# How the per-token scales of a quantized FFN reach all partitions: a row in DRAM and two DMAs, in place of diagonal matrices

## The chip, the cores and the metric

The program runs on one core of a Trainium2 chip. TensorE (PE) multiplies and transposes, VectorE (DVE), ScalarE (ACT) and GpSimd (POOL) do elementwise work, and SyncE (SP) issues all DMAs of this kernel. The metric is the device time of one launch, in microseconds.

## The reference

64 sequences of 128 tokens, 256 features. A cross-attention block with 16 heads, then a feed-forward block whose two linear layers take inputs quantized to 8 bits per token and ternary weights.

```python
def act_quant(x):
    scale = 127.0 / jnp.clip(jnp.max(jnp.abs(x), axis=-1, keepdims=True), 1e-05)
    return jnp.clip(jnp.round(x * scale), -128, 127) / scale
...
    h = bit_linear(x, w1)                       # 256 -> 1024
    h = depthwise_conv1d(h.transpose(0, 2, 1), conv_w, conv_b)
    h = h.transpose(0, 2, 1)
    h = jax.nn.silu(h)
    return bit_linear(h, w2)                    # 1024 -> 256
...
x = x + xattn(_layernorm(x), ctx_768, ...)
x = x + ffn(_layernorm(x), ...)
```

The scale of `act_quant` is one number per token. The kernel computes it where tokens lie on partitions (a tile of 128 partitions by 4 sequences), but it needs it where tokens lie along the free axis, on every partition alike: the hidden layer is kept transposed, hidden channel on the partition and 4 x 128 = 512 tokens along the row.

## The kernel before, in words

The 64 sequences are worked on in 16 groups of 4. The work of one group is cut into 32 half-steps, numbered `n` 0 to 31 (and on from 32 where it runs over into the next group's time). Each engine has one long instruction stream, written out by hand: at half-step `n` of loop index `g` it does a piece of the attention of group `g` (`attend`, `scores`, `exponentials`), of the projections of group `g+1` (`project`), and of the feed-forward block of groups `g-1` and `g-2` (`finish`, called with `n` and with `n + 32`). Engines meet only through semaphores, and each runs its stream in order, SP's queue of DMA issues too. Loop indices 0, 1, 15, 16 and 17 are written out, 2 to 14 (13 of them) are a hardware loop, whose body is the same program.

The scale of the first linear layer: DVE computes `AD[0]` and `AS[0]` in `scales` at half-step 10. `AD[0]` is then made into four diagonal matrices (`DIAG`, line 761), PE multiplies a matrix of ones with them into PSUM at half-step 14 (line 497), ACT copies the result into `BC` (line 666) at half-step 15, and DVE multiplies each of the eight hidden tiles by `BC` (line 862) from half-step 15 on. PSUM bank `psF` is shared by all of `finish`, so the first matmul of the first layer (line 505) waits for that copy.

The scale of the second layer: at half-step 30 DVE reads the maxima that PE has transposed (line 876), computes `AS[1]` (line 758) and again the diagonal matrices; PE multiplies at half-step 32 (line 514), ACT copies at 33, and at half-steps 33 to 35 DVE (line 883) and POOL (line 1038) multiply the eight tiles of `H` by `BC`, DVE rounds them (line 890), and PE starts the second layer's matmuls (line 524).

Two loads matter for the change. The input `XIN` of the group after next is issued by SP at half-step 0 (line 311), when `unit_full` says that the previous `XIN` has been read; DVE needs it in the same half-step 0 (`bn_stats`, line 769), which stands ahead of line 883 in DVE's stream. The residual input `XRES` is issued at half-step 12 (line 333) and read by POOL from half-step 16 on (line 1065).

Of the kernel before, what the change touches and what calls it, by code (L numbers as in the profile page):

```python
# [27 lines left out]
P = 128  # L28
# [40 lines left out]
M_POW, M_NORM = 9, 9  # L69
M_QT, M_BC1 = 13, 14  # L70
M_F1 = 15
# [3 lines left out]
M_HMAX = M_F1 + M_TILE[-1] + M_HOFF  # L75
M_HT, M_BC2 = M_HMAX + 2, M_HMAX + 4
M_Q2 = M_HMAX + 5
# [57 lines left out]
def program(nc, x, ctxT, cipaT, Wq, Wk, Wv, Wo, bo, q_downT, q_up, k_downT, k_up, v_downT, v_up, o_downT, o_up,  # L135
            alphas, Wk_ipa, Wv_ipa, w1T, conv_w, conv_b, w2T, out):
    with ExitStack() as ctx:
# [66 lines left out]
        OUTT = H[:, 0:NB, T // 2:T]  # L204
        DIAG, HM = GB[0], GB[1]

# [39 lines left out]
        q1_scaled, q1_done = sem("q1_scaled"), sem("q1_done")  # L246
        diag_done = sem("diag_done")
        q1t_full, q1t_done, bc_full, bc_done = (sem(n) for n in ("q1t_full", "q1t_done", "bc_full", "bc_done"))
        f1_full, g_done, t1_done, t2_done, t3_done, th_done, h_done = (
# [52 lines left out]
        def _(sp):  # L302
# [83 lines left out]
        def _(pe):  # L386
# [98 lines left out]
            def finish(g, n):  # L485
                if n == M_QT:
# [6 lines left out]
                    m.then_inc(q1t_full, 1)  # L493
                if n == M_BC1:
                    pe.wait_ge(diag_done, g.count(2, 1))
                    pe.wait_ge(q1t_done, g.count(1, 1))
                    mm(psF, ONES[:].broadcast_to([P, P]), DIAG.rearrange("p b t -> p (b t)"), start=True, stop=True).then_inc(bc_full, 1)
                j = tile_at(n - M_F1)
                if 0 <= j < CT:
                    if j == 0:  # L500
                        pe.wait_ge(bc_done, g.count(2, 1))
                    else:
                        pe.wait_ge(g_done, g.count(CT, j))
                    for k in range(2):
                        m = mm(psF, W1[:, k, P * j:P * j + P], Q1T[:, k, :], start=(k == 0), stop=(k == 1))  # L505
                    m.then_inc(f1_full, 1)
                if n == M_HT:
# [3 lines left out]
                    m.then_inc(ht_full, 1)  # L511
                if n == M_BC2:
                    pe.wait_ge(diag_done, g.count(2, 2))
                    mm(psF, ONES[:].broadcast_to([P, P]), DIAG.rearrange("p b t -> p (b t)"), start=True, stop=True).then_inc(bc_full, 1)
                for c in range(2):
# [82 lines left out]
        def _(act):  # L598
# [53 lines left out]
            def finish(g, n):  # L652
# [3 lines left out]
                if n == M_COPY:  # L656
                    act.wait_ge(q2_done, g.count(CT, NB))
                    act.activation(OUTT, X2[:], ACT.Identity).then_inc(copy_done, 1)
                for c, m in enumerate((M_BC1 + 1, M_BC2 + 1)):
                    if n == m:  # L660
                        act.wait_ge(bc_full, g.count(2, c + 1))
                        if c == 0:
                            need(act, q2_done, g.count(CT, 0))
                        else:
                            act.wait_ge(g_done, g.count(CT, CT))
                        act.activation(BC[:], psF, ACT.Identity).then_inc(bc_done, 1)
                j = tile_at(n - M_F1 - M_LAG[0])
# [59 lines left out]
        def _(dve):  # L727
# [20 lines left out]
            def scales(g, i, clip, levels, worth):  # L748


                step = lambda k: dve.wait_ge(quant[i], g.count(4, k))
                step(1)
                dve.tensor_scalar(AM[i][:], AR[i][:], clip, None, ALU.max).then_inc(quant[i], 1)
                step(2)
                dve.tensor_scalar(AD[i][:], AM[i][:], worth, WD[:, i:i + 1], ALU.mult, ALU.mult)
                dve.reciprocal(AR[i][:], AM[i][:]).then_inc(quant[i], 1)
                step(3)
                dve.tensor_scalar(AS[i][:], AR[i][:], levels, None, ALU.mult).then_inc(quant[i], 1)
                step(4)
                for b in range(NB):  # L760
                    m = dve.tensor_scalar(DIAG[:, b, :], IDF[:], (AD if i == 0 else AS)[i][:, b:b + 1], None, ALU.mult)
                m.then_inc(diag_done, 1)

# [43 lines left out]
            def finish(g, n):  # L807
# [27 lines left out]
                if n == M_NORM + M_SCALE:  # L835
                    need(dve, h_done, g.count(CT, 0))
                    scales(g, 0, CLIP, 127.0, 1.0 / 127.0)
# [18 lines left out]
                if 0 <= j < CT:  # L856
                    dve.wait_ge(f1_full, g.count(CT, j + 1))
                    if j == 0:
                        dve.wait_ge(bc_done, g.count(2, 1))
                    if j >= 4:  # L860
# [17 lines left out]
                for j in range(CT):  # L878
                    if n == M_Q2 + j // 3 and j % 3 < 2:
                        dve.wait_ge(bc_done, g.count(2, 2))  # L880
                        if j >= 4:
# [109 lines left out]
        def _(pool):  # L991
# [37 lines left out]
            def finish(g, n):  # L1029
# [3 lines left out]
                for j in range(CT):  # L1033
                    if n == M_Q2 + j // 3 and j % 3 == 2:
                        pool.wait_ge(bc_done, g.count(2, 2))
                        if j >= 4:
# [76 lines left out]
```

## Time and profile before

| | us |
|---|---|
| median of 3 runs | 1683.01 |
| lowest and highest | 1680.71 to 1685.13 |
| span of the profiled execution | 1677.3 |

The span goes from the first to the last instruction; the times of whole runs are taken around it and lie 3.4 to 7.8 above it. The profile's own rows, below, give for each engine the time in which it was busy, the chain of work that ended last, and, for one group, the instructions in order of time. The loop's groups repeat each other closely, so one is read for all.

### The profile page before, as it was taken

How to read it: one execution, taken by the hardware profiler on the slowest of the kernel's cores; microseconds unless marked ns; L12 is line 12 of the kernel's file. 1: busy time of each engine (PE TensorE's matmuls, PEld its weight loads, DVE VectorE, ACT ScalarE, POOL GpSimd, SP SyncE). 2: the span in 40 equal slices, each digit the busy share in tenths (PEclk: the TensorE clock that was granted, in tenths of full speed). 3: DMA queues.
4: the chain of work that ended last, by engine and by line, in shares of the span. 5: the costliest groups of instructions: out<-in, count | busy, mean ns of one | idle time of the engine just before them, and what ended most of it. 6: DMA issues, size and time to landing. Idle time of an engine off the chain costs nothing.

```text
span 1677.3 us, 33155 instructions
## 1 busy us (share of the span) xinstructions
PE 1469.8 (88%) x10540; PEld 1161.8 (69%) x10586; DVE 1310.7 (78%) x3159; ACT 1183.0 (71%) x3925; POOL 729.7 (44%) x1086
## 2 busy tenths in 40 slices
PE   6999998989899998989999998989999898998642
PEld 2578877777777777777777777777777777776521
DVE  5254698887879888887979888787988888787976
ACT  2277786968778696867778696877869686776621
POOL 0125444454444544453444444444454445444510
PEclk8699999999999999999999999999999999999955
DMA  6300100000010100000010000001010000000000
GB/s 186 116 28 15 29 15 28 15 26 27 13 39 13 40 13 27 14 26 27 13 40 13 28 13 26 27 13 39 13 40 13 27 13 26 27 1 27 1 13 13
DMA packets 41128, 47.13 MB, mean 28 GB/s; under 512 B 3008, under 2 KB 35200, under 8 KB 41088
## 3 DMA queue, kind: packets, MB, share of 16 engines
q1 hardware_dynamic: 41088, 46.62, 9.1%
q8 instruction: 22, 0.36, 0.1%
q14 instruction: 18, 0.15, 0.0%
HBM read 36.13 MB, written 10.49 MB: 28 GB/s over the span
## 4 chain that ended last, share of the span: by engine, by line
PE 34%; DVE 33%; ACT 20%; issue 12%; SPq 1%; DMA 0%; DVEq 0%; POOL 0%; ACTq 0%; POOLq 0%
ACT SM L647 8%; DVE GBS L872 7%; PE PS L467 6%; PE PS L429 4%; PE PS L445 4%; PE PS L524 4%; PE PS L410 4%; PE PS L454 3%; PE PS L480 3%; PE PS L419 3%; DVE GBS L883 2%; ACT H L672 2%; DVE GBS L862 2%; ACT GBS L677 2%; DVE H L890 2%
## 5 line engine op out<-in xcount | busy, mean ns | idle before, releaser
L1026 POOL TENSOR_TENSOR SM<-SM,RC 128x496 f32<-128x496 f32 (+1 forms) x512 | 337.0, 679 | 728.8 <-DVE RC L798 728.8
L647 ACT ACTIVATE SM<-PS,MX 128x124 f32<-128x124 f32 x1024 | 359.2, 365 | 199.3 <-DVE SM L804 196.1
L467 PE MATMUL PS<-KT,QM 128*128 128x128 f32 x2048 | 279.2, 279 | 26.4 <-ACT SM L647 26.3
L467 PEld LDWEIGHTS PS<-KT,QM 128*128 128x128 f32 x2048 | 249.3, 192 | 42.6 <-ACT SM L647 41.5
L1058 POOL TENSOR_TENSOR OTl<-OF,OTh 128x256 fp32r<-128x256 f32 x256 | 216.1, 844 | 5.6 <-ACT OF L641 5.6
L647 ACT ACTIVATION_READ_ACCUMULATOR SM<-PS,MX 128x1 f32 x1024 | 210.8, 206 | 0.0
L454 PE MATMUL PS<-IDF,SM 128*128 128x128 f32 x1024 | 168.5, 287 | 18.8 <-POOL SM L1026 18.8
L639 ACT ACTIVATE OTh<-PS 128x256 fp32r<-128x256 f32 x256 | 99.5, 389 | 101.8 <-PE PS L445 98.1
L802 DVE TENSOR_REDUCE MX<-PS 128x4 f32<-128x496 f32 x256 | 170.2, 665 | 0.0
L445 PE MATMUL PS<-PT,V 128*64 128x128 f32 x2048 | 168.8, 286 | 0.0
L445 PEld LDWEIGHTS PS<-PT,V 128*64 128x64 f32 x2048 | 106.8, 136 | 82.4 <-issue 75.5
L633 ACT ACTIVATE PT<-PS 128x512 f32<-128x512 f32 x256 | 155.6, 608 | 0.1
L454 PEld LDWEIGHTS PS<-IDF,SM 128*128 128x128 f32 x1024 | 107.8, 141 | 65.0 <-issue 35.4
L480 PE MATMUL PS<-WOh,OTh 128*128 128x256 f32 x512 | 124.6, 325 | 18.3 <-POOL OTl L1058 18.3
L862 DVE TENSOR_TENSOR GBS<-PS,BC 128x512 f32<-128x512 f32 x128 | 87.6, 684 | 61.0 <-PE PS L505 58.3
L672 ACT ACTIVATE H<-GBS,CB,CW 128x512 f32<-128x512 f32 x128 | 105.4, 823 | 29.9 <-DVE GBS L862 28.6
L801 DVE TENSOR_REDUCE MX<-PS 128x4 f32<-128x16 f32 x256 | 41.3, 161 | 107.7 <-PE PS L467 107.7
L867 DVE SCALAR_TENSOR_TENSOR H<-GBS,H 128x512 f32<-128x512 f32 x128 | 106.0, 828 | 24.5 <-ACT GBS L677 24.4
L641 ACT ACTIVATE OF<-PS 128x256 f32<-128x256 f32 x256 | 99.4, 388 | 31.2 <-POOL OTl L1058 31.2
L872 DVE TENSOR_REDUCE GBS<-H 128x128 f32<-128x1024 f32 x64 | 120.3, 1923 | 0.0
L847 DVE SCALAR_TENSOR_TENSOR H<-GBS,CW,H 128x508 f32<-128x508 f32 x128 | 116.8, 913 | 0.0
L853 DVE SCALAR_TENSOR_TENSOR H<-GBS,CW,H 128x508 f32<-128x508 f32 x128 | 108.3, 846 | 10.3 <-ACT H L672 8.7
(145 smaller groups left out, 3685.4 us busy)
## 6 DMA issues: line engine op xcount, KB each, us to landing
XIN<-in_x SPq DMA_DIRECT2D x16, 512.0 KB, 3.5
XRES<-in_x SPq DMA_DIRECT2D x16, 512.0 KB, 3.5
out_y<-H SPq DMA_DIRECT2D x16, 512.0 KB, 3.0
CRAW<-in_ctxT SPq DMA_DIRECT2D x16, 256.0 KB, 2.7
RRAW<-in_ctxT SPq DMA_DIRECT2D x32, 128.0 KB, 3.0
QM<-in_Wq SPq DMA_DIRECT2D x1, 1024.0 KB, 6.2
GBS<-in_Wo SPq DMA_DIRECT2D x1, 1024.0 KB, 12.9
k_ipa_columns<-H SPq DMA_DIRECT2D x1, 1024.0 KB, 5.2
```

The costliest lines, as they stand in the source:

```text
L445: m = mm(psO[r:r + DH, h // 2, :], V[:, b, DH * (4 * q + h):DH * (4 * q + h) + DH], PT[:, h, :], start=True, stop=True)
L454: m = pe.transpose(psT[:, h, :], SM[c % 2][:, h, :], IDF[:])
L467: m = mm(psS[:, h, :], QM[:, 2 * q + h // 2, h % 2, TOK * b:TOK * b + TOK], KT[:, 2 * q + h // 2, b, :], start=True, stop=True)
L480: m = mm(psY[b // 2][:, b % 2, :], OT[ot][c % 2][:, a, :], WO[w][:, 2 * q + a, :], start=(q == 0 and i == 0 and b % 2 == 0), stop=(q == QU ...
L633: act.activation(PT[:], psT, ACT.Identity).then_inc(pt_done, 1)
L647: m = act.activation(SM[s % 2][:, h, 0:ORG], psS[:, h, 0:ORG], ACT.Exp, bias=MX[s % 2][:, h:h + 1], accum_out=SU[s % 2][:, h:h + 1])
L672: act.activation(H[:, j, :].rearrange("p (b t) -> p b t", b=NB), GB[j % 4], ACT.Identity, bias=CB[:, j:j + 1], scale=CW[:, j, 1:2]).then_i ...
L802: dve.tensor_reduce(MX[s % 2][:, 0:4], psS[:, :, 0:ORG], AX.X, ALU.max, negate=True)
L862: dve.tensor_tensor(GB[j % 4].rearrange("p b t -> p (b t)"), psF, BC[:], ALU.mult).then_inc(g_done, 1)
L872: dve.tensor_reduce(HM[:, b, :], H[:, :, TOK * b:TOK * b + TOK].rearrange("p j t -> p t j"), AX.X, ALU.max, apply_absolute_value=True).the ...
L1026: m = pool.tensor_tensor(part, part, RC[c % 2][:, 4 * i:4 * i + 4].unsqueeze(2).broadcast_to(shape), ALU.mult)
L1058: pool.tensor_tensor(OT[1][c % 2][:], OF[:], OT[0][c % 2][:].bitcast(F32), ALU.subtract).then_inc(ot_done, 1)
```

## The change

Diagonal matrices, the product with ones and ACT's copy are gone, for both layers. Instead SP writes the 512 scales from the tile (128 partitions by 4) into a row in DRAM, waits for that, and reads the row back to all 128 partitions, into `BC`. The first pair of DMAs is issued at half-step 11 (`M_ROW1`), the second at half-step 30 (`M_HT`). The users of `BC` wait for the second DMA of each pair.

```diff
-M_QT, M_BC1 = 13, 14
+M_QT = 13
+M_ROW1 = 11
...
-M_HT, M_BC2 = M_HMAX + 2, M_HMAX + 4
+M_HT = M_HMAX + 2
...
+            def spread_scale(g, i, tile):
+                sp.wait_ge(row_ready[i], g.count(1, 1))
+                sp.dma_start(row_dram[i].rearrange("b t -> t b"), tile[:], allow_slow_non_contiguous=True).then_inc(row_out[i], 16)
+                sp.wait_ge(row_out[i], g.count(16, 16))
+                sp.dma_start(BC[:], row_dram[i].rearrange("(o b) t -> o (b t)", o=1).broadcast_to([P, T])).then_inc(bc_in[i], 16)
+
             def finish(g, n):
+                if n == M_ROW1:
+                    need(sp, q2_done, g.count(CT, 0))
+                    spread_scale(g, 0, AD[0])
+                if n == M_HT:
+                    sp.wait_ge(g_done, g.count(CT, CT))
+                    spread_scale(g, 1, AS[1])
...
-                if n == M_BC1:
-                    pe.wait_ge(diag_done, g.count(2, 1))
-                    pe.wait_ge(q1t_done, g.count(1, 1))
-                    mm(psF, ONES[:].broadcast_to([P, P]), DIAG.rearrange("p b t -> p (b t)"), start=True, stop=True).then_inc(bc_full, 1)
                 j = tile_at(n - M_F1)
                 if 0 <= j < CT:
                     if j == 0:
-                        pe.wait_ge(bc_done, g.count(2, 1))
+                        pe.wait_ge(q1t_done, g.count(1, 1))
...
-                if n == M_BC2:
-                    pe.wait_ge(diag_done, g.count(2, 2))
-                    mm(psF, ONES[:].broadcast_to([P, P]), DIAG.rearrange("p b t -> p (b t)"), start=True, stop=True).then_inc(bc_full, 1)
...
-                        act.activation(BC[:], psF, ACT.Identity).then_inc(bc_done, 1)
...
-                step(4)
-                for b in range(NB):
-                    m = dve.tensor_scalar(DIAG[:, b, :], IDF[:], (AD if i == 0 else AS)[i][:, b:b + 1], None, ALU.mult)
-                m.then_inc(diag_done, 1)
...
                     if j == 0:
-                        dve.wait_ge(bc_done, g.count(2, 1))
+                        dve.wait_ge(bc_in[0], g.count(16, 16))
...
-                        dve.wait_ge(bc_done, g.count(2, 2))
+                        dve.wait_ge(bc_in[1], g.count(16, 16))
...
-                        pool.wait_ge(bc_done, g.count(2, 2))
+                        pool.wait_ge(bc_in[1], g.count(16, 16))
```

SP's queue before, from half-step 11 of the loop body to its end (the next row to run is the loop's first, the load of `XIN`):

```order
L327 DMA V<-v_ipa_rows 4x4x256 [waits o_full]
L333 ISA [waits x2_done]
L333 DMA XRES<-in_x 128x4x256
...
L327 ISA [waits o_full]
L327 DMA V<-v_ipa_rows 4x4x256
L127 REGISTER_ALU
L127 COMPARE_AND_BRANCH
```

The same stretch of SP's queue after the change:

```order
L339 DMA scale_row<-AD 128x4x1 [waits row_ready0,q2_done]
L341 DMA BC<-scale_row 128x512 [waits row_out0]
L335 ISA [waits x2_done]
L335 DMA XRES<-in_x 128x4x256
...
L329 DMA V<-v_ipa_rows 4x4x256
L339 DMA scale_row<-AS 128x4x1 [waits row_ready1,g_done]
L341 DMA BC<-scale_row 128x512 [waits row_out1]
L128 REGISTER_ALU
L128 COMPARE_AND_BRANCH
```

The first pair stands ahead of the load of `XRES`, the second behind the last load of `V` in the body and so, in time, ahead of the next load of `XIN`, which is the first DMA of the loop's body both before and after.

DVE's stream before, from the scale of the second layer at half-step 30 to the first products with `BC` at 33 (`SU`, `RC` and `MX` belong to the attention of the next group):

```order
L758 TENSOR_SCALAR AS<-AR 128x4 [waits quant1]
L761 TENSOR_SCALAR GBS<-IDF,AS 128x128 [waits quant1]
L761 TENSOR_SCALAR GBS<-IDF,AS 128x128 x3
...
L804 TENSOR_TENSOR SM<-PS,MX 128x4x4 [waits max_done]
L767 REGISTER_ALU
L769 BN_STATS BS<-XIN 128x6 [waits x_in]
L769 BN_STATS BS<-XIN 128x6
L880 ISA
L883 TENSOR_TENSOR GBS<-H,BC 128x512 [waits bc_done] x2
```

And after:

```order
L759 TENSOR_SCALAR AS<-AR 128x4 [waits quant1]
...
L803 TENSOR_TENSOR SM<-PS,MX 128x4x4 [waits max_done]
L766 REGISTER_ALU
L768 BN_STATS BS<-XIN 128x6 [waits x_in]
L768 BN_STATS BS<-XIN 128x6
L878 REGISTER_ALU
L881 TENSOR_TENSOR GBS<-H,BC 128x512 [waits bc_in1] x2
```

The four diagonal products are gone; the statistics of `XIN` still stand ahead of the first use of `BC`, which now waits for a DMA.

## Rows read from the trace of the kernel before

**Rows 1.** The page: busy time by engine, and the chain that ended last.

```profile
PE 1469.8 (88%) x10540; PEld 1161.8 (69%) x10586; DVE 1310.7 (78%) x3159; ACT 1183.0 (71%) x3925; POOL 729.7 (44%) x1086
...
PE 34%; DVE 33%; ACT 20%; issue 12%; SPq 1%; DMA 0%; DVEq 0%; POOL 0%; ACTq 0%; POOLq 0%
```

**Rows 2.** The chain through one group, 657 to 753 us: start, us, what.

```profile
675.50 0.88 DVE GBS L761 x4
...
679.23 1.50 ACT SM L647 x8
...
685.54 0.61 ACT BC L666
...
735.69 0.17 DVE MX L801
...
738.17 0.50 ACT BC L666
...
749.36 1.92 PE PS L524 x16
```

**Rows 3.** PE in order of time, 680 to 687 us: start, us; idle before in brackets.

```profile
680.77 1.16 PE L467 MATMUL PS<-KT,QM 128*128 128x128 f32 x8 [0.31 <-ACT SM L647]
...
683.88 1.02 PE L497 MATMUL PS<-GBS,ONES 128*128 128x512 f32 x2
684.34 0.80 PE L419 MATMUL PS<-CTh,WKh 128*128 128x512 f32 x1
684.97 0.39 PE L419 MATMUL PS<-CTl,WKh 128*128 128x512 f32 x1
...
686.42 0.38 PE L505 MATMUL PS<-Q1T,W 128*128 128x512 bf16 x1 [0.35 <-ACT BC L666]
```

**Rows 4.** DVE in order of time, the same group.

```profile
674.62 0.23 DVE L755 TENSOR_SCALAR AD<-AM,WD 128x4 f32<-128x4 f32 x1
...
686.92 0.69 DVE L862 TENSOR_TENSOR GBS<-PS,BC 128x512 f32<-128x512 f32 x1 [3.52 <-PE PS L505]
...
734.38 0.17 DVE L758 TENSOR_SCALAR AS<-AR 128x4 f32<-128x4 f32 x1
...
736.45 0.74 DVE L769 BATCH_NORM_STATS2 BS<-XIN 128x6 f32<-128x256 f32 x2
738.69 2.37 DVE L883 TENSOR_TENSOR GBS<-H,BC 128x512 f32<-128x512 f32 x2 [1.50 <-ACT BC L666]
740.98 1.61 DVE L890 TENSOR_SCALAR H<-GBS 128x512 bf16<-128x512 f32 x3
```

**Rows 5.** Tile BC: the operations that read it, ns least/median/most.

```profile
L883 DVE TENSOR_TENSOR GBS<-H,BC x96: 676/694/1765, 261.0 to 1665.2; 128x512 f32<-128x512 f32 x96
L1038 POOL TENSOR_TENSOR GBS<-H,BC x32: 1309/1590/1781, 261.1 to 1661.3; 128x512 f32<-128x512 f32 x32
```

**Rows 6.** SP's DMA issues in order of time: start, us to issue.

```profile
675.30 0.38 SPq L333 DMA_DIRECT2D XRES<-in_x  x1
...
720.47 0.27 SPq L327 DMA_DIRECT2D V<-v_ipa_rows  x1
721.37 0.40 SPq L311 DMA_DIRECT2D XIN<-in_x  x1
```

**Rows 7.** DMA issues by line: count, KB each, median us to landing.

```profile
XIN<-in_x SPq DMA_DIRECT2D x16, 512.0 KB, 3.5
...
CRAW<-in_ctxT SPq DMA_DIRECT2D x16, 256.0 KB, 2.7
...
RRAW<-k_ipa_columns SPq DMA_DIRECT2D x16, 64.0 KB, 2.0
```

**Rows 8.** POOL in order of time: the first read of XRES.

```profile
683.19 0.74 POOL L1065 TENSOR_TENSOR XRES<-XRES,BO 128x256 f32<-128x256 f32 x1
688.01 1.19 POOL L1026 TENSOR_TENSOR SM<-SM,RC 128x496 f32<-128x496 f32 x2 [4.08 <-DVE RC L798]
```

**Rows 9.** The last group, in order of time, with nothing else running.

```profile
1617.46 2.04 PE L497 MATMUL PS<-GBS,ONES 128*128 128x512 f32 x2 [1.21 <-ACT Q1T L655]
...
1621.27 0.69 DVE L862 TENSOR_TENSOR GBS<-PS,BC 128x512 f32<-128x512 f32 x1 [6.10 <-PE PS L505]
...
1654.20 0.17 DVE L758 TENSOR_SCALAR AS<-AR 128x4 f32<-128x4 f32 x1
...
1658.08 2.36 DVE L883 TENSOR_TENSOR GBS<-H,BC 128x512 f32<-128x512 f32 x2 [2.80 <-ACT BC L666]
```

More of the change, by code:

```diff
@@ L204, in program @@
         OUTT = H[:, 0:NB, T // 2:T]
-        DIAG, HM = GB[0], GB[1]
+        HM = GB[1]
         PS = ctx.enter_context(nc.psum_tensor("PS", [P, 8, 512], F32))
@@ L246, in program @@
         q1_scaled, q1_done = sem("q1_scaled"), sem("q1_done")
-        diag_done = sem("diag_done")
-        q1t_full, q1t_done, bc_full, bc_done = (sem(n) for n in ("q1t_full", "q1t_done", "bc_full", "bc_done"))
+        row_ready, row_out, bc_in = ([sem(f"{n}{i}") for i in range(2)] for n in ("row_ready", "row_out", "bc_in"))
+        q1t_full, q1t_done = sem("q1t_full"), sem("q1t_done")
         f1_full, g_done, t1_done, t2_done, t3_done, th_done, h_done = (
@@ L258, in program @@
         vipa_dram = nc.dram_tensor("v_ipa_rows", [SEQS * IPA, ID], F32, kind="Internal").ap()
+        row_dram = [nc.dram_tensor(f"scale_row{i}", [NB, TOK], F32, kind="Internal").ap() for i in range(2)]
         kipa_dram = nc.dram_tensor("k_ipa_columns", [GROUPS, P, PAIRS * NB * IPA], F32, kind="Internal").ap()
@@ L658, in finish @@
                     act.activation(OUTT, X2[:], ACT.Identity).then_inc(copy_done, 1)
[L659 to L665, printed above, removed]
-                        act.activation(BC[:], psF, ACT.Identity).then_inc(bc_done, 1)
                 j = tile_at(n - M_F1 - M_LAG[0])
@@ L748, in scales @@
             def scales(g, i, clip, levels, worth):
-                step = lambda k: dve.wait_ge(quant[i], g.count(4, k))
+                step = lambda k: dve.wait_ge(quant[i], g.count(4 - i, k))
                 step(1)
@@ L754, in scales @@
                 step(2)
-                dve.tensor_scalar(AD[i][:], AM[i][:], worth, WD[:, i:i + 1], ALU.mult, ALU.mult)
+                m = dve.tensor_scalar(AD[i][:], AM[i][:], worth, WD[:, i:i + 1], ALU.mult, ALU.mult)
+                if i == 0:
+                    m.then_inc(row_ready[0], 1)
                 dve.reciprocal(AR[i][:], AM[i][:]).then_inc(quant[i], 1)
                 step(3)
-                dve.tensor_scalar(AS[i][:], AR[i][:], levels, None, ALU.mult).then_inc(quant[i], 1)
-                step(4)
-                for b in range(NB):
-                    m = dve.tensor_scalar(DIAG[:, b, :], IDF[:], (AD if i == 0 else AS)[i][:, b:b + 1], None, ALU.mult)
-                m.then_inc(diag_done, 1)
+                dve.tensor_scalar(AS[i][:], AR[i][:], levels, None, ALU.mult).then_inc(quant[0] if i == 0 else row_ready[1], 1)
+                if i == 0:
+                    step(4)
             def project(g, n):
@@ L835, in finish @@
                 if n == M_NORM + M_SCALE:
-                    need(dve, h_done, g.count(CT, 0))
                     scales(g, 0, CLIP, 127.0, 1.0 / 127.0)
```

## The prediction, made before the changed kernel had run

> **What bounds the kernel now.** I read first the busy shares and the chain of work that ended last [rows 1]. PE is busy 88% of the span, but holds only 34% of the chain; DVE holds 33% and ACT 20%. So no engine is the bound by itself. The reader should see three engines handing one another work, and must ask at each place of the change which of them comes last there. Second I read the chain through one group, since the groups of the loop repeat [rows 2]. Of what the change removes, three pieces stand on it: DVE's diagonal matrices at 675.50, ACT's copy at 685.54, and ACT's copy at 738.17. PE's product for the second layer isn't on it. Third, the engines in order of time around these places [rows 3, 4], to see how far behind the second in line is. Last, SP's queue [rows 6], since the change puts two waits into it.
>
> **First layer (half-steps 10 to 15): a gain.**
> - Diagonal matrices: four operations, 0.88 us by the chain; the next operation starts 0.78 after. They lead through DVE's scores' maxima to ACT's exponentials at 679.23 and to PE's scores at 680.77 [rows 2, 3]. There PE was idle for only 0.31 us, so it is itself nearly late. The cover gone, 0.78 off DVE is worth 0.31.
> - The product with ones: PE starts it at 683.88; the first matmul of line 419 follows at 684.34 with 0.80 where its like takes 0.39 to 0.40, and the second starts at 684.97. Matmuls of this shape start some 0.23 apart, so without the product the second would start at 684.11: 0.86 off PE, which works without a gap from 680.77 to 686.42 [rows 3].
> - ACT's copy: the first matmul of line 505 waited 0.35 for it [rows 3]. It now needs only the transposed input, copied long before. 0.35 off.
> - Sum: 0.31 + 0.86 + 0.35 = 1.5 us a group. All of DVE (3.52 idle before line 862) and, behind line 445, ACT were waiting for PE here [rows 4], so they move with it.
> - The new DMAs: the scale is ready at 674.85 [rows 4]. SP is then free (it issued a load at 675.30 [rows 6]). With the prices below, row out at 675.3, landed 678.1, read back issued at 678.2, landed at 680.9. It is needed at 686.9 - 1.5 = 685.4 [rows 4]: hidden, with 4.5 us to spare. The price is nil unless the pair takes 10 us.
> - What is queued behind: the load of XRES goes from 675.30 to about 678.8 and lands at 678.8 + 3.5 = 682.3 [rows 6, 7]. POOL reads it at 683.19, and after two short operations waits 4 us for other work [rows 8]: nil.
>
> **Prices of the new transfers.** No row shows 512 pieces of 4 bytes written to DRAM. The nearest are a 64 KB load in 128 pieces, 2.0 us to landing, and the 512 KB load of XIN, which has 512 pieces as well, of 1 KB, 3.5 us [rows 7]. I take the middle, 2.8 us, as it has as many pieces as the second and fewer bytes than either; bounds 1.8 and 4.2, the second because writes of single elements to DRAM may cost more each than 1 KB reads. The read back has the shape of CRAW's load, 128 rows of 2 KB: 2.7 us [rows 7], bounds 2.0 and 3.5, since all rows come from one place. The page DMA: Bandwidth & Descriptors of the Trainium skill (Rules for kernel authors) says that a strided last dimension becomes one descriptor per element and advises against it; it gives no price for this case. In its section Anatomy of one DMA, fitted to another issuing path, it has a fixed cost of about 2.0 us, mostly the receipt of the write. With 2.0 for the row, the estimate by that page would be 13 us lower than mine.
>
> **Second layer (half-steps 30 to 33): a loss.** This is the place that decides.
> - The scale AS is ready at 734.38 + 0.17 = 734.55 [rows 4]. SP has nothing to issue at that time and waits: row out at 734.7, landed at 737.5, read back issued at 737.65, landed at 740.35. Before, BC was there at 738.67 [rows 2], and DVE began line 883 at 738.69, having waited 1.50 [rows 4]. By BC alone: 1.66 us later.
> - The diagonal matrices that go (0.78) give nothing here: DVE's next maxima wait for PE's scores and started at 735.69 behind them [rows 2]. PE's product isn't on the chain either.
> - The step that the change doesn't show in its own lines: SP's queue is in order. The load of XIN was issued at 721.37, 15 us before DVE read it at 736.45 [rows 4, 6]. Now it stands behind the wait for the scale and the wait for the row, and is issued after the read back, at about 738.4 (issue 0.35 to 0.4, and the loop's end). It lands 3.5 us later, plus some 0.2 for the read back ahead of it in the same queues: 742.1. DVE's statistics of XIN wait for it from 736.45, and line 883 is behind them: 742.1 + 0.74 = 742.85, instead of 738.69. That is 4.15 us late.
> - What comes back: line 883's first two took 2.37 us with POOL's line 1038 beside them; alone one takes 0.68 to 0.69 [rows 4, 5]. POOL doesn't wait for XIN, starts at 740.35 and is through (1.31 alone, 1.6 in the median) before DVE starts. So 2.37 becomes 1.35: 1.0 back.
> - 4.15 - 1.0 = 3.1 us a group. From 738.69 to the second layer's matmuls at 749.36 [rows 2] DVE works almost without a gap and PE waits 0.45 for it, so the delay is passed on in full.
>
> **Sum.** The loop has 13 turns in which XIN is loaded behind the second pair: 13 x 3.1 = +40. Two more groups have no XIN behind the pair: 2 x 1.66 = +3.3. The first layer gains in 15 groups beside attention: 15 x 1.5 = -22.5. The last group is alone [rows 9]. First layer: line 862 ran at 1621.27; the read back lands about 5.7 us after the scale, at 1617.9, and PE's first matmul can start at 1616.7 instead of behind the product at 1617.46: -3.3. Second: the scale at 1654.37, BC at 1654.37 + 5.7 = 1660.0 instead of 1658.08: +2.0. Together -1.3. In all +40.3 + 3.3 - 22.5 - 1.3 = +20 us. On the profiled execution's span: 1677.3 + 20 = 1697. The median of the runs is 5.7 above that span; with the same distance: 1703 us, 1.2% slower.
>
> **Rivals.**
> - *Faster.* The row and the read back are quick. One microsecond off the row is worth 13 + 2 + 1 = 16 us over the program. At 1.2 us for the row the sum is -5.6: 1677. From there on it is faster. No row of the trace lands in less than 1.8 us, and that is against it; that the row is only 2 KB is for it. Chance 9%.
> - *About the same.* The row in 1.25 to 1.85 us, or 2.0 together with a first-layer gain of 2 us a group (all of DVE's 0.78, PE's 0.86 and the 0.35 counting): 20 - 13 - 7.5 = 0, 1683. Chance 11%.
> - *Only BC is late, XIN is hidden.* If the order in SP's queue didn't matter, the second layer would cost 15 x 1.66 = 25, the first gain 22.5: 1684. The queue's order speaks against it, and so does DVE's stream, in which the statistics stand ahead of line 883. It is part of the 11%.
> - *Much slower.* The 512 single elements take 4.2 us or more: 1703 + 16 x 1.4 = 1725 and up. For it speaks that nothing in the trace writes such pieces. Part of the chance for slower, 80%; I give this end 15%.
>
> **How the numbers follow.** The likeliest case gives 1703. A measurement of this kernel tells about 0.3% (5 us) from no change. The bounds of the row (1.8 to 4.2) give 1687 to 1725; first-layer gains of 0.9 to 2.1 and the XIN landing 0.5 off add some 10 in squares. With the case of about the same just touched, 1686 to 1728 leaves out two in ten. Slower 0.80, same 0.11, faster 0.09.
>
> **What would show it.** In the changed kernel's profile: DVE's line for the statistics of XIN idle some 5.5 us before it, released by the DMA of XIN, in 13 groups; line 883's successor without a wait of its own there, with a mean near 0.7 for the first two; SP's issue of XIN 4 us behind AS; PE's first matmul of line 505 without wait, and line 862 waiting for PE and not for BC; the period of a group longer by 1.6 us. It would be wrong if XIN's wait is short (a quick row), if DVE waits for BC at half-step 15 (a row over 7 us), or if PE's 1.2 us of the first layer turn up as idle time before its next instruction.

## The result, and the profile after

| | before | after |
|---|---|---|
| median, us | 1682.01 (4 runs) | 1873.84 (4 runs) |
| lowest and highest | 1680.71 to 1685.13 | 1868.53 to 1875.45 |
| span of the profiled execution | 1677.3 | 1873.1 |
| TensorE's mean granted clock | 0.965 | 0.899 |

The ratio is 1.113, 95% interval 1.110 to 1.115: 191.8 us slower. The direction was as forecast. The size wasn't: 1873.8 lies far above the range of 1686 to 1728.

The page after, where [rows 1] show before: busy time by engine, then the chain that ended last, by engine and by line.

```profile
PE 1510.3 (81%) x10522; PEld 1203.8 (64%) x10522; DVE 1244.0 (66%) x3031; ACT 1167.6 (62%) x3893; POOL 720.0 (38%) x1086
...
PE 26%; DVE 23%; DMA 21%; ACT 15%; issue 12%; POOL 2%; SPq 1%; ACTq 0%; DVEq 0%; POOLq 0%
DMA scale_row<-AS 7%; DVE GBS L870 6%; DMA scale_row<-AD 6%; DMA BC<-scale_row 5%; ACT SM L654 4%; PE PS L424 4%; PE PS L481 4%; DMA XIN<-in_x 3%; PE PS L531 3%; PE PS L433 3%; PE PS L459 3%; DVE GBS L860 2%; PE PS L494 2%; DVE GBS L881 2%; PE PS L443 2%
```

DMA held 0% of the chain before and holds 21% now. Both writes of the row are on it, the first layer's (`AD`) as well, which the prediction had as hidden. How long each took shows in the chain through one group (start, us, what):

```profile
737.81 8.34 DMA scale_row<-AD
746.16 5.16 DMA BC<-scale_row
...
797.83 8.78 DMA scale_row<-AS
...
807.64 5.47 DMA XIN<-in_x
```

The row takes 8.3 to 8.8 us, against a price of 2.8 and an upper bound of 4.2; the read back takes 5.2 against 2.7. DVE's wait for `BC` in the first layer, which the prediction named as a sign of being wrong, is there in all 16 groups (108.1 us below, line 860). The engines wait for the transfers as follows (us in total, times, longest):

```profile
POOL GBS L1036 <- DMA BC<-scale_row: 241.2, 16, 62.5
DVE BS L768 <- DMA XIN<-in_x: 161.4, 14, 13.4
POOL XRES L1063 <- DMA XRES<-in_x: 122.8, 15, 8.9
DVE GBS L860 <- DMA BC<-scale_row: 108.1, 16, 11.1
```

DVE around the second layer, where [rows 4] show before:

```profile
797.59 0.17 DVE L759 TENSOR_SCALAR AS<-AR 128x4 f32<-128x4 f32 x1
...
800.87 0.16 DVE L803 TENSOR_TENSOR SM<-PS,MX 128x16 f32<-128x16 f32 x1
813.13 0.75 DVE L768 BATCH_NORM_STATS2 BS<-XIN 128x6 f32<-128x256 f32 x2 [12.11 <-DMA XIN<-in_x]
813.80 1.28 DVE L881 TENSOR_TENSOR GBS<-H,BC 128x512 f32<-128x512 f32 x2
```

The shape is the forecast one. The wait stands at the statistics of `XIN` and not at `BC`, and the first two products take 1.28 us where they took 2.37, as POOL is through by then. Only the wait is 12.11 us. Attention runs dry meanwhile. The windows of that stretch (us; busy time of PE, PEld (its weight loads), DVE, ACT and POOL; granted clock; busy share of the DMA engines; GB/s) show it:

```profile
796.00:800.00 4.00, 4.00 (x32) 3.70 (x32) 1.90 (x7) 3.34 (x14) 2.37 (x5) 0.77 0.06 1
800.00:806.00 6.00, 4.34 (x34) 3.42 (x32) 0.83 (x3) 2.36 (x11) 0.00 (x0) 1.00 0.00 0
806.00:812.00 6.00, 0.00 (x0) 0.00 (x0) 0.00 (x0) 0.00 (x0) 0.22 (x1) 0.67 0.54 111
812.00:818.00 6.00, 4.22 (x17) 3.28 (x19) 4.83 (x15) 2.12 (x5) 3.90 (x4) 0.50 0.06 20
```

From 806 to 812 no engine but POOL does anything. The granted clock falls there and is at 0.50, the lower of its two levels (1.2 GHz), when TensorE starts again.

All kernels below but e7 are compared by the same stages of a group: mean lengths in us over nine groups of the loop, worked out from DVE's and PE's rows in order of time. A is from the start of `AD`'s operation in the second layer's `scales` (0.34 before that of `AS`) to the first product of `H` with `BC`; B from there to the second layer's first matmul; C from `AD`'s operation in the first layer to the first product with `BC`; D from there to the first maximum over the hidden tiles. The two stages left out, from that maximum to `AD` (10.4) and from the second layer's matmuls to the next `AD` (20.8), are the same in all of them to 0.05.

| kernel | A | B | C | D | period |
|---|---|---|---|---|---|
| before | 4.79 | 10.67 | 12.31 | 36.68 | 95.68 |
| after | 16.39 | 9.03 | 14.59 | 36.32 | 107.55 |
| e1 row in 16-byte pieces | 8.78 | 11.82 | 10.48 | 38.33 | 100.64 |
| e2 loads first | 13.79 | 11.15 | 14.92 | 36.51 | 107.60 |
| e3 first layer only | 5.83 | 10.66 | 14.81 | 36.12 | 98.65 |
| e4 second layer only | 16.65 | 9.03 | 12.22 | 36.87 | 106.01 |
| e5 reads an old row | 15.11 | 9.03 | 13.60 | 35.57 | 104.54 |
| e6 reads 128 rows | 15.36 | 9.36 | 13.37 | 35.50 | 104.82 |
| e8 first layer, copied | 5.83 | 10.67 | 10.48 | 36.76 | 94.97 |
| e9 the same, with filler | 4.64 | 10.67 | 10.48 | 36.76 | 93.83 |
| e10 pieces 512 B apart | 8.08 | 9.34 | 10.47 | 36.76 | 95.86 |
| e11 pieces 16 B apart | 8.97 | 9.47 | 10.47 | 36.76 | 96.88 |
| e12 pieces 64 B apart | 8.14 | 9.02 | 10.47 | 36.76 | 95.61 |

A group is 11.87 us longer after the change: A +11.60, C +2.28, B -1.64, D -0.36.

### The profile page after: what moved, and what is told of

Read it like the earlier page. It is cut to its first block, busy times and chain, and to the rows that moved or that the text cites. A ratio compares the mean times of both kernels' runs of the same rounds, so it can differ in the third digit from the quotient of the medians.

```text
span 1873.1 us, 32959 instructions
## 1 busy us (share of the span) xinstructions
PE 1510.3 (81%) x10522; PEld 1203.8 (64%) x10522; DVE 1244.0 (66%) x3031; ACT 1167.6 (62%) x3893; POOL 720.0 (38%) x1086
## 4 chain that ended last, share of the span: by engine, by line
PE 26%; DVE 23%; DMA 21%; ACT 15%; issue 12%; POOL 2%; SPq 1%; ACTq 0%; DVEq 0%; POOLq 0%
DMA scale_row<-AS 7%; DVE GBS L870 6%; DMA scale_row<-AD 6%; DMA BC<-scale_row 5%; ACT SM L654 4%; PE PS L424 4%; PE PS L481 4%; DMA XIN<-in_x 3%; PE PS L531 3%; PE PS L433 3%; PE PS L459 3%; DVE GBS L860 2%; PE PS L494 2%; DVE GBS L881 2%; PE PS L443 2%
## 5 line engine op out<-in xcount | busy, mean ns | idle before, releaser
L481 PE MATMUL PS<-KT,QM 128*128 128x128 f32 x2048 | 287.9, 285 | 21.8 <-ACT SM L654 21.7
L481 PEld LDWEIGHTS PS<-KT,QM 128*128 128x128 f32 x2048 | 260.8, 199 | 34.6 <-ACT SM L654 33.2
L1056 POOL TENSOR_TENSOR OTl<-OF,OTh 128x256 fp32r<-128x256 f32 x256 | 204.3, 798 | 5.6 <-ACT OF L648 5.6
L468 PE MATMUL PS<-IDF,SM 128*128 128x128 f32 x1024 | 178.0, 299 | 11.7 <-POOL SM L1024 11.6
L494 PEld LDWEIGHTS PS<-WOh,OTh 128*128 128x128 f32 x512 | 83.5, 205 | 153.5 <-POOL OTl L1056 153.5
L459 PE MATMUL PS<-PT,V 128*64 128x128 f32 x2048 | 180.5, 300 | 0.0
L459 PEld LDWEIGHTS PS<-PT,V 128*64 128x64 f32 x2048 | 114.6, 144 | 88.8 <-issue 83.1
L860 DVE TENSOR_TENSOR GBS<-PS,BC 128x512 f32<-128x512 f32 x128 | 87.4, 682 | 114.1 <-DMA BC<-scale_row 108.1
L1036 POOL TENSOR_TENSOR GBS<-H,BC 128x512 f32<-128x512 f32 x32 | 43.8, 1368 | 271.2 <-DMA BC<-scale_row 241.2
L515 PE MATMUL PS<-Q1T,W 128*128 128x512 bf16 x256 | 84.5, 415 | 71.4 <-DVE GBS L860 69.5
L768 DVE BATCH_NORM_STATS2 BS<-XIN 128x6 f32<-128x256 f32 x64 | 23.6, 414 | 161.4 <-DMA XIN<-in_x 161.4
```

The source lines that it names most:

```text
L459: m = mm(psO[r:r + DH, h // 2, :], V[:, b, DH * (4 * q + h):DH * (4 * q + h) + DH], PT[:, h, :], start=True, stop=True)
L468: m = pe.transpose(psT[:, h, :], SM[c % 2][:, h, :], IDF[:])
L481: m = mm(psS[:, h, :], QM[:, 2 * q + h // 2, h % 2, TOK * b:TOK * b + TOK], KT[:, 2 * q + h // 2, b, :], start=True, stop=True)
L494: m = mm(psY[b // 2][:, b % 2, :], OT[ot][c % 2][:, a, :], WO[w][:, 2 * q + a, :], start=(q == 0 and i == 0 and b % 2 == 0), stop=(q == QU ...
L860: dve.tensor_tensor(GB[j % 4].rearrange("p b t -> p (b t)"), psF, BC[:], ALU.mult).then_inc(g_done, 1)
L1056: pool.tensor_tensor(OT[1][c % 2][:], OF[:], OT[0][c % 2][:].bitcast(F32), ALU.subtract).then_inc(ot_done, 1)
```

## The experiments

**e1, the row in 16-byte pieces.** Each partition's four scales are written as they lie, 128 pieces of 16 bytes in place of 512 of 4. The products then read `BC` with a stride of four elements.

```diff
-row_dram = [nc.dram_tensor(f"scale_row{i}", [NB, TOK], F32, kind="Internal").ap() for i in range(2)]
+row_dram = [nc.dram_tensor(f"scale_row{i}", [TOK, NB], F32, kind="Internal").ap() for i in range(2)]
...
-sp.dma_start(row_dram[i].rearrange("b t -> t b"), tile[:], allow_slow_non_contiguous=True).then_inc(row_out[i], 16)
+sp.dma_start(row_dram[i], tile[:]).then_inc(row_out[i], 16)
...
+BC_BT = BC[:].rearrange("p (t b) -> p b t", b=NB)
...
-dve.tensor_tensor(GB[j % 4].rearrange("p b t -> p (b t)"), psF, BC[:], ALU.mult).then_inc(g_done, 1)
+dve.tensor_tensor(GB[j % 4], psF.rearrange("p (b t) -> p b t", b=NB), BC_BT, ALU.mult).then_inc(g_done, 1)
```

> The row is stored token by token, so that each partition writes its four scales as one piece of 16 bytes: 128 pieces in place of 512 of 4 bytes. The read back is the same 2 KB row to all partitions; its users read it with a stride of 16 bytes. Theory A (the row is slow because of its 512 single elements): it lands in 2 to 3 us instead of 8.3 to 8.8, the second layer's first product with BC is about 5 us late instead of 12, the first layer's transfers are hidden, and the time is 1715 to 1745 us. Theory B (the time is the latency of a write to DRAM that is waited for, whatever its pieces): it stays at 8 us or more, and the time at 1865 to 1880. An unknown beside it: what the stride costs DVE and POOL in the products.

Measured: 1764.6 us, ratio 1.047 (1.044 to 1.050). SP issues the read back as soon as the row has landed, so the distance of the two issues is the row's time:

```profile
764.36 0.35 SPq L340 DMA_DIRECT2D scale_row<-AS  x1
765.83 0.35 SPq L342 DMA_DIRECT2D BC<-scale_row  x1
766.84 0.39 SPq L314 DMA_DIRECT2D XIN<-in_x  x1
```

1.47 us instead of 8.8, and 109 us of the 192 come back. The mechanism was right, the expected time 20 to 50 us too low, for a cost that I had not counted: the stride. DVE's lines for the products (count, busy, mean ns):

```profile
L861 DVE TENSOR_TENSOR GBS<-PS,BC 128x512 f32<-128x512 f32 x128 | 137.2, 1072 | 42.6 <-PE PS L516 39.2 <-DMA BC<-scale_row 3.4
L882 DVE TENSOR_TENSOR GBS<-H,BC 128x512 f32<-128x512 f32 x96 | 117.1, 1259 | 13.5 <-DMA BC<-scale_row 13.5
```

A product with unit stride takes 684 ns, here 1072. Each element now lies 16 bytes behind the last. By the page SBUF — State Buffer of the Trainium skill (Door 1: The DMA port swizzle) 4 fp32 is where the reach of a free stride ends; the 388 ns are what this operation pays at it. That the line is the reason isn't shown: no run takes another stride. Stages B (+2.8 against the same stage after) and D (+2.0) hold it. C is 10.48: with a quick row the first layer's transfers are hidden and the gain there is 1.83.

**e2, the loads first.** The loads of `XRES` and `XIN` are issued ahead of the pairs, everything else as after.

```diff
-M_ROW1 = 11
+M_ROW1 = 12
...
-                if n == M_HT:
-                    sp.wait_ge(g_done, g.count(CT, CT))
+                if n == M_HT + 2:
                     spread_scale(g, 1, AS[1])
```

> Only SP's order is changed: the loads of XIN and XRES stand ahead of the pair of scale transfers that they stood behind. Theory A (the loads behind the read back share the DMA engines with it and slow it): the read back of the second layer lands in about 3.4 us, as in the last group, instead of 5.1; DVE no longer waits for XIN, but about 9.5 us for BC; 2.6 us a group in the second layer and 1 to 2 in the first: 1810 to 1835 us. Theory B (the read back is slow of itself, by its one row): it stays at 5.1, and the gain is only what XIN lands behind it, 1850 to 1865. If the queue's order were the main cause of the loss, as the prediction had it, the time would come to about 1700.

Measured: 1878.5 us, ratio 1.116 (1.111 to 1.121), no better than after and above both ranges expected. With no load behind it the read back lands in 4.7 us, between the two theories' 3.4 and 5.1. The order in SP's queue, on which the prediction laid most weight, isn't the bound at these durations: `XIN` in time takes 2.6 off A, and B grows by 2.1, since DVE's and POOL's products then start together. `XRES` now lands in 3.5 us instead of 6.1, and C and D together are 51.4 against 50.9 after, so the late `XRES` cost nothing that these stages show.

**e3 and e4, one layer alone.** The other layer keeps diagonal matrices, product and copy. The diff is e3's against after, cut to SP and PE; e4 does the same with `M_ROW1` and `M_BC1`.

```diff
-                if n == M_HT:
-                    sp.wait_ge(g_done, g.count(CT, CT))
-                    spread_scale(g, 1, AS[1])
...
+                if n == M_BC2:
+                    pe.wait_ge(diag_done, g.count(1, 1))
+                    mm(psF, ONES[:].broadcast_to([P, P]), DIAG.rearrange("p b t -> p (b t)"), start=True, stop=True).then_inc(bc_full, 1)
```

> Only the first layer's scale goes by DMA, the second's by diagonal matrices, product and copy as before. Theory: BC arrives 2 us after the place where it is needed, less 1.5 us that the removed work gives back on PE; 0.7 us a group by the trace of the changed kernel, and 5 us in the last group: 1690 to 1705 us. Rival (the load of XRES, late behind the pair, stops POOL and costs more than DVE's wait): 1720 or more.

> Only the second layer's scale goes by DMA. Theory: 10 to 12 us a group in the 13 groups with XIN behind the pair, 8 in two more and 9 in the last: 1835 to 1860 us. Rival (both layers share the loss, 6 us each): 1770 to 1785. If the costs of e3 and e4 add up to less than 190 us, the rest belongs to what both do together, such as TensorE's clock after long waits.

Measured: the first layer alone 1737.0 us, ratio 1.031 (1.028 to 1.034); the second alone 1849.0, 1.096 (1.093 to 1.100). The second layer holds most of the loss, as forecast. The first layer, forecast as a gain of 22.5, is a loss of 52. That is 32 us above the range expected of e3 and in that of its rival; but e2 speaks against the rival's reason, the late `XRES`. DVE's line for its products, in the kernel with only that layer changed:

```profile
L868 DVE TENSOR_TENSOR GBS<-PS,BC 128x512 f32<-128x512 f32 x128 | 87.4, 683 | 115.5 <-DMA BC<-scale_row 111.8 <-PE PS L513 1.9
```

The two losses, 52 and 163 against the runs of before beside them, add up to 215 instead of 192. Most of the difference stands in the table: e3 has C +2.50 and D -0.56, but also A +1.04, in a stage of the second layer that it doesn't touch. In 12 of its 14 groups with attention beside them the second layer's products start 5.8 us after `AS` instead of 4.3, and the granted clock falls around it, as in this window (`AS` at 658.36):

```profile
657.00:661.00 4.00, 4.00 (x26) 3.44 (x25) 2.58 (x11) 3.34 (x14) 2.12 (x5) 0.59 0.00 0
```

That is 12 x 1.5 = 18 us of e3's 52. With both layers changed, A waits for the DMAs anyway, and they don't come on top. e8 and e9 take this up.

**e5 and e6, what the read back reads.** To part the row's age from its form, the read back takes the first 2 KB of the input, 2 KB that nobody has written in this launch (e5), or 128 different rows of the input (e6). The row is written as before and nobody reads it, so the products get wrong scales and only the times count. In the diff e5's line stands first, then e6's.

```diff
-sp.dma_start(BC[:], row_dram[i].rearrange("(o b) t -> o (b t)", o=1).broadcast_to([P, T])).then_inc(bc_in[i], 16)
+sp.dma_start(BC[:], x.rearrange("s t d -> (s t d)").rearrange("(o n) -> o n", n=T)[0:1, :].broadcast_to([P, T])).then_inc(bc_in[i], 16)
+sp.dma_start(BC[:], x.rearrange("s t d -> (s t d)").rearrange("(o n) -> o n", n=T)[0:P, :]).then_inc(bc_in[i], 16)
```

> The changed kernel, with the read back taken from the first 2 KB of the input x in place of the scale row (its values are not the scales, so the output is another). The row is written and waited for as before. Theory A (the read back takes 5 us because all 128 pieces come from one 2 KB row, whichever): landing stays at 4.5 to 5.2 us and the time at 1865 to 1880. Theory B (it is slow because the row has just been written): 2.7 to 3.2 us, and 1835 to 1850.

> As e5, but each partition reads a row of its own, 128 different rows of 2 KB of the input x (again not the scales). Theory A (one row for all is what is slow): landing falls to CRAW's 2.7 us, XIN's with it, and the time to 1825 to 1850. Rival (the loads behind it or the engines' traffic slow it): it stays near 5.

Measured, one run each: 1835.5 and 1831.7 us, both as expected of the second theory of e5 and the first of e6; but the landings expected there, 2.7 to 3.2 and 2.7, did not come. DMA issues of after, then of e5 and of e6 (count, KB each, median us to landing):

```profile
XIN<-in_x SPq DMA_DIRECT2D x16, 512.0 KB, 5.7
XRES<-in_x SPq DMA_DIRECT2D x16, 512.0 KB, 6.1
BC<-scale_row SPq DMA_DIRECT2D x32, 256.0 KB, 5.1
```

```profile
XIN<-in_x SPq DMA_DIRECT2D x16, 512.0 KB, 4.2
XRES<-in_x SPq DMA_DIRECT2D x16, 512.0 KB, 5.0
BC<-in_x SPq DMA_DIRECT2D x32, 256.0 KB, 3.8
```

```profile
XIN<-in_x SPq DMA_DIRECT2D x16, 512.0 KB, 4.4
XRES<-in_x SPq DMA_DIRECT2D x16, 512.0 KB, 4.9
BC<-in_x SPq DMA_DIRECT2D x32, 256.0 KB, 3.8
```

Reading an old row back takes 3.8 us instead of 5.1, and `XIN`, next in the queue, gains 1.5. One row for all 128 partitions or 128 rows makes no difference. So reading back the row just written costs 1.3 us more, and with what it does to `XIN` that is worth 38 us. Its age and its place in DRAM changed together here. How it was written counts as well: read back just after it was written in 16-byte pieces (e1), it lands in 4.3. The row's write stays at 8.6. Why 128 rows of `x` take 3.8 where `CRAW`, of the same shape, takes 2.7 isn't shown in full.

**e7, e10, e11, e12, how far apart the pieces lie.** As e5, with the 512 four-byte pieces spread in DRAM: 512 B, 64 B or 16 B from one to the next instead of 4. Their number and size stay. The diff is that of e7 and e10; e12 has 16 in place of 128, e11 has 4.

```diff
-row_dram = [nc.dram_tensor(f"scale_row{i}", [NB, TOK], F32, kind="Internal").ap() for i in range(2)]
+row_dram = [nc.dram_tensor(f"scale_row{i}", [NB, TOK, 128], F32, kind="Internal").ap() for i in range(2)]
...
-sp.dma_start(row_dram[i].rearrange("b t -> t b"), tile[:], allow_slow_non_contiguous=True).then_inc(row_out[i], 16)
+sp.dma_start(row_dram[i].rearrange("b t k -> t b k")[:, :, 0], tile[:], allow_slow_non_contiguous=True).then_inc(row_out[i], 16)
```

> As e5 (so to be compared with e5), and the row's 512 single elements are written 512 bytes apart in DRAM instead of side by side. Theory A (the cost is per piece): the row lands in 8 to 9.5 us as before, 1865 to 1880 us. Theory B (the cost is that many engines write into the same 512 bytes of DRAM): it lands in 2 to 4 us, and the time falls to 1745 to 1790, as the row's does in e1.

The one execution of e7 took 2321.3 us with TensorE at a granted clock of 0.556 from its beginning on, so its time isn't comparable; the row landed in 1.8 us. e10 is the same kernel: its ten executions took 1679 to 1690 us. e11 and e12 have smaller distances.

> The kernel of the pieces 512 B apart once more (it reads the first 2 KB of the input back in place of the row, so its scales are not the reference's), since its first time fell into an execution with TensorE at half clock. With the row written in 1.8 us and the data back in 3.9, the two transfers cost 5.7 us together, about the 5.5 of the prediction. If the prediction's working was right but for its prices: AS to the products of the second layer 8 us, the first layer's transfers hidden (AD to the first product about 10.5), time 1690 to 1710. Rival, that the change has further costs which the prediction left out (a late XIN or XRES, TensorE's clock): above 1715.

> As the one before, each 4-byte piece 16 B after the last instead of 512 B (again the first 2 KB of the input are read back). If what is slow is several pieces inside one small block of DRAM, of 64 B or more, the row still takes well above 1.8 us: 3 to 8. If only pieces that touch are slow: 1.8 us. Time 1690 to 1710 for the fast row, up to 1835 for the slow one.

> As the one before with 64 B from piece to piece. If the block is 64 B: row 1.8 us and the time of the 512 B kernel within 3 us. If the block is larger (512 B): still 2.5 to 5 us for the row and a time between that kernel and 1835.

| distance of the pieces | row, median us to landing | time, us | ratio to before |
|---|---|---|---|
| 4 B (e5) | 8.6 | 1835.5 | one run |
| 16 B (e11) | 2.6 | 1699.0 | 1.010 (1.008 to 1.011) |
| 64 B (e12) | 1.8 and 1.9 | 1686.0 | 1.002 (1.001 to 1.003) |
| 512 B (e10) | 1.8 | 1683.8 | 1.001 (1.000 to 1.002) |

The row's lines in the DMA view of e11, e12 and e10:

```profile
scale_row<-AD SPq DMA_DIRECT2D x16, 2.0 KB, 2.6
scale_row<-AS SPq DMA_DIRECT2D x16, 2.0 KB, 2.6
```

```profile
scale_row<-AD SPq DMA_DIRECT2D x16, 2.0 KB, 1.8
scale_row<-AS SPq DMA_DIRECT2D x16, 2.0 KB, 1.9
```

```profile
scale_row<-AD SPq DMA_DIRECT2D x16, 2.0 KB, 1.8
scale_row<-AS SPq DMA_DIRECT2D x16, 2.0 KB, 1.8
```

So the count of pieces costs almost nothing (1.8 us for 512 of them, 1.5 for e1's 128). What costs 6.8 us is that the 4-byte pieces lie close together; at 64 B from one to the next the cost is gone. Touching alone isn't it: e1's 16-byte pieces touch and take 1.5, while e11's 4-byte pieces start as far apart, don't touch and take 2.6. e10's time lies 6 us below the foot of its expectation. e12 is within 3 us of it, as expected for a quick row. e11's 2.6 us stand between the two cases set out for it: 512 pieces, four to each 64 B, still cost 0.8 us, and the kernel's time is the one expected of a quick row. The page DMA: Bandwidth & Descriptors of the Trainium skill (Specifications) says that transfers under 512 B are done by read-modify-write. Pieces that wait for each other's read-modify-write in one small block would fit the table (4-byte pieces: 16, 4 and 1 of them in 64 B); by the table the block would be 64 B or less. No run here shows the mechanism itself, and e1's pieces, quick at four to a block, need a further reason, such as their smaller number.

**e8, the best of both.** Only the first layer goes by DMA, in 16-byte pieces, where there is time. It is read back into a free buffer, and POOL, idle there, makes the unit-stride copy into `BC`. `XRES` is loaded ahead of the pair. The second layer is as before.

```diff
+                sp.dma_start(BCT, row_dram[i].rearrange("(o t) b -> o (t b)", o=1).broadcast_to([P, T])).then_inc(bc_in[i], 16)
...
+                if n == M_F1:
+                    pool.wait_ge(bc_in[0], g.count(16, 16))
...
+                    pool.tensor_copy(BC[:].rearrange("p (b t) -> p b t", b=NB), BCT.rearrange("p (t b) -> p b t", b=NB)).then_inc(bc_flat[0], 1)
```

> The first layer's scale alone goes by DMA, in 16-byte pieces, into a buffer, from which POOL makes the copy in the order that DVE's products want, so that they keep their unit stride; XRES is loaded ahead of the pair. The second layer is as before. Theory: row 1.5 us, read back 3 to 5, copy 1 to 2, in all under the 10.5 us from the scale to its first use, so only the removed work is left: 1.5 to 1.8 us a group for 15 groups, 1655 to 1663 us. Rival (POOL's wait and copy hold up its attention work or share DVE's path to memory): 1675 to 1690.

Measured: 1669.3 us, ratio 0.992 (0.991 to 0.994): faster than before by less than 1%, and 6 us short of the expectation. The row behind the load of `XRES` lands in 3.2 us, where 1.5 was expected, but with the read back's 3.6 and the copy's 1.1 still in time:

```profile
scale_row<-AD SPq DMA_DIRECT2D x16, 2.0 KB, 3.2
```

C gives 1.83 a group, but A takes 1.04 back, in a stage that this kernel doesn't touch. In 12 of the 14 groups with attention beside them, line 891 started 5.8 us after `AS`, in the other two 4.31, as before. PE in order of time, once in a group of each kind:

```profile
634.85 0.65 PE L520 MATMUL PS<-IDF,GBS 128*128 128x128 f32 x4 [2.20 <-DVE GBS L880]
...
636.85 1.12 PE L459 MATMUL PS<-PT,V 128*64 128x128 f32 x8
637.91 1.12 PE L468 MATMUL PS<-IDF,SM 128*128 128x128 f32 x4
638.82 1.46 PE L481 MATMUL PS<-KT,QM 128*128 128x128 f32 x8
```

```profile
730.17 0.66 PE L520 MATMUL PS<-IDF,GBS 128*128 128x128 f32 x4 [2.20 <-DVE GBS L880]
...
731.93 0.66 PE L459 MATMUL PS<-PT,V 128*64 128x128 f32 x8
732.52 0.66 PE L468 MATMUL PS<-IDF,SM 128*128 128x128 f32 x4
733.01 1.06 PE L481 MATMUL PS<-KT,QM 128*128 128x128 f32 x8
```

The same matmuls take 1.12 and 0.66. The windows say why: PE is idle 2.20 us for DVE's maxima, and in the first of the two groups the granted clock falls 1.4 us after it has started again.

```profile
632.00:636.00 4.00, 1.80 (x13) 1.34 (x12) 3.97 (x8) 0.12 (x1) 0.81 (x1) 1.00 0.00 0
636.00:640.00 4.00, 4.00 (x25) 3.44 (x25) 2.69 (x11) 3.55 (x14) 2.12 (x5) 0.57 0.00 0
...
727.00:731.00 4.00, 1.80 (x12) 1.28 (x11) 3.96 (x6) 0.00 (x0) 0.49 (x1) 1.00 0.00 0
731.00:735.00 4.00, 4.00 (x36) 3.50 (x35) 3.83 (x17) 3.61 (x15) 2.12 (x4) 1.00 0.00 0
```

**e9, the same with the gap filled.** Eight products of constants go into `psF` while PE waits; the transposes overwrite their result.

```diff
                 if n == M_HT:
+                    pe.wait_ge(g_done, g.count(CT, CT))
+                    for _ in range(8):
+                        mm(psF, W1[:, 0, 0:P], W1[:, 1, 0:512], start=True, stop=True)
                     pe.wait_ge(hm_done, g.count(NB, NB))
```

> As the 16-byte copy for the first layer, with eight products more into psF (two constant pieces of W1, 128x512, result overwritten by the transposes that follow) while TensorE waits for the maxima over the hidden tiles. Theory: the 16-byte copy kernel gave back most of its gain because TensorE stands idle 2.20 us there and its granted clock then falls to 0.57 for some 4 us in 12 of 14 groups, where AS to the products of the second layer takes 5.83 instead of 4.31 us; with the wait filled the clock stays at 1.00, every group is like its two fast ones (period 93.8 instead of 95.3), and the time is 1669 - 12 x 1.5 = 1651 (1647 to 1657). Rival, that the 1.5 us come from an order of waits that has nothing to do with the clock: 1669 or up to 10 us more for the added products, with 5.83 us still there.

Measured: 1651.3 us, ratio 0.981 (0.980 to 0.982), as expected to a microsecond. PE and the windows at the same place of the group (the second row is the filler):

```profile
625.36 0.39 PE L433 MATMUL PS<-CTR,WKRl 128*128 128x512 f32 x1
625.60 1.90 PE L520 MATMUL PS<-W 128*128 128x512 bf16 x8
628.01 0.66 PE L523 MATMUL PS<-IDF,GBS 128*128 128x128 f32 x4 [0.51 <-DVE GBS L883]
...
629.77 0.66 PE L459 MATMUL PS<-PT,V 128*64 128x128 f32 x8
```

```profile
625.10:629.10 4.00, 3.49 (x21) 1.98 (x20) 3.97 (x8) 0.07 (x1) 0.75 (x1) 1.00 0.00 0
629.10:633.10 4.00, 4.00 (x36) 3.42 (x34) 3.83 (x16) 3.82 (x16) 2.13 (x5) 1.00 0.00 0
```

Line 894 starts 4.30 us after `AS` in all 14 groups, and the period is 93.83.

## Why the size was wrong, point by point

**The step that failed** is the price of the row: "I take the middle, 2.8 us [...] bounds 1.8 and 4.2". It measured 8.3 to 8.8. I priced it by its count of pieces and its bytes, from loads, in pieces of 512 B and 1 KB. e10 shows that this part was even generous: 512 pieces of 4 bytes, apart, take 1.8. What no row of before showed was 4-byte pieces written side by side in DRAM. The upper bound of 4.2 had no row behind it; "at least 1.8, and nothing above it known" would have been honest. The second price was off too, the read back's 2.7 with bounds of 2.0 and 3.5. `CRAW`, from which it was taken, still lands in 2.8. The read back takes 3.8 even from rows that nobody has just written, and in e6 it has `CRAW`'s own shape; the just-written row brings it to 5.1. Part of it is the load behind it in the queue: with none behind, it took 3.6 in e8 against e1's 4.3, both from a row just written in 16-byte pieces. It is part of the reason that `XIN`, behind it, took 5.5 to 5.7 instead of 3.7.

The rival *Much slower*, given 15%, is the case that came, for the reason that stood beside it. Its own sum gives 1703 + 16 x 5.8 = 1796 for a row of 8.6 us. An estimate of the rest from the rows: `XIN` lands some 2 us later still in 13 groups, and the first layer loses 1.9 instead of gaining 1.5 in 15, 26 + 51 us, which comes near the measured time.

**The working around the prices held.** e11 has a row of 2.6 us, near to the 2.8 of the forecast, and a read back of 3.8: it took 1699.0 us, where the prediction has 1703. There DVE waits for `XIN` 62.1 us in 13 groups, 4.8 each, forecast 5.5; C is 1.84 shorter, forecast 1.5; B 1.2 shorter, forecast 1.0. The rival *about the same*, for a row of 1.25 to 1.85 us, is e10: 1683.8. "One microsecond off the row is worth 16 us" was 19 from e10 to e11, and 23 from e11 to e5, where the first layer's pair is no longer hidden.

**Second layer.** Forecast: line 883 4.15 late, 1.0 back, 3.1 a group. Measured: `AS` to line 881 16.21 us in the group shown instead of 4.31, so 11.9 late. The difference of 7.7 is the row (6.0), the landing of `XIN` (1.8) and little else. B gave back 1.64. Over the groups 9.96 instead of 3.1.

**First layer.** The gain was there: 1.83 a group in e8 to e12, wherever the transfers are hidden. "The price is nil unless the pair takes 10 us" was right as a condition. The pair took 8.34 + 5.16 = 13.5, so 4.1 us of C came on top of the gain: +1.9 a group instead of -1.5. So the first layer's sign was wrong, by the same price. The late `XRES` was nil as forecast, though POOL waited 122.8 us for it: that wait stood beside DVE's for `BC`, and e2, where it is gone, is no faster.

**The sum.** By the starts of `AS`, the loop's 13 periods took 155.4 us more than before, 12.0 each against 1.6 forecast; the last two groups 27.3 more; the end behind the last `AS` 9.4; the start 3.8. Together that is the span's 195.8. In the last group nothing covers the waits, and the row and the read back take their full 13 us from the scale to line 881, where product and copy took 3.9.

**TensorE's clock.** The prediction left it out. In the changed kernel it falls to 0.50 in the long wait of stage A, as shown above for one group, and stage B is shorter than before all the same; its cost there wasn't parted from the rest. In e8 it is 1.5 us in 12 groups, and e9 shows that: 18 us by eight products that compute nothing. e3 has it in 12 groups too. The page TensorE: Matmul & The Clock Gate of the Trainium skill (HAM oscillation — how this bites in real kernels) describes waits for DMA, longer than this one, that throttle the clock again each time; e8's trace agrees in part, 0.57 in the 4 us that follow, but not each time. Why it fell in 12 groups of e8 and in one of 14 before stays open: PE's idle time there is the same to 0.01 us (2.21 before), and its busy time in the windows too. The trace gives one hint. In successive groups of e8 the fall comes 0.35, 0.58, 0.86, 1.12 and 1.40 us after PE has started again, then there is a group without one, then it comes after 0.03, 0.29 and so on. So it seems to hang on when the wait comes, and not on its length; no run tests that.

## What to carry to other kernels

Look at how a DMA's pieces lie in DRAM before counting them: 4-byte pieces side by side took 8.6 us, the same pieces 64 B apart 1.8 to 1.9, and the same bytes in pieces of 16 B 1.5. Where the trace has no row of the kind, the upper bound isn't known, and the range has to say so. A round trip through DRAM (here 1.5 + 4.3 us in e1, 3.2 + 3.6 in e8) paid where the value isn't needed for longer than that, as in the first layer, and cost time where the next engine waits for it, as in the second. When a gain comes short in a stage that the edit doesn't touch, look at the duration of the same matmuls and at the granted clock; filling a wait of 2 us on TensorE was worth 18 us here, more than the 13 that the best form of the change (e8) gave.

## What the runs showed of the hardware that was not expected

- A DMA of 512 four-byte pieces into DRAM lands in 8.6 us with the pieces side by side, 2.6 at 16 B, 1.8 to 1.9 at 64 B and 1.8 at 512 B; 128 pieces of 16 B side by side land in 1.5 to 1.6 (e1), and in 3.2 with the load of `XRES` ahead of them in the queue (e8).
- A 2 KB row of DRAM read to 128 partitions lands in 3.8 us when it is an old row of the input, and in 5.1 when it is the row written just before in 4-byte pieces; 128 different rows take the same 3.8. Written in 16-byte pieces it lands in 4.3 (e1), and with no load behind it in the queue in 3.6 (e8).
- The load that follows in the queue lands later as well: `XIN` 3.5 us alone, 4.2 behind an old row, 4.9 behind a new one in 16-byte pieces, 5.7 behind a new one in 4-byte pieces.
- DVE's 128x512 product takes 684 ns, and 1072 when one operand in SBUF has a stride of 16 bytes.
- A wait of 2.20 us on TensorE went with a fall of its granted clock to 0.50 in 12 of 14 groups of e8 and in one of 14 before; with the wait filled there was none (e9).
